# A decoder layer on one core: where TensorE's background jobs stand against the sum of the state in each round of the scan

## The chip, the core and the metric

The kernel runs on one core of one Trainium2 chip. The metric is the device time of one execution in microseconds. The core has TensorE (matmuls and transposes), VectorE, ScalarE, GpSimd and SyncE (which here only issues transfers). Each engine works through its own instructions in order, and they meet through semaphores.

## The reference, cut to what matters

Four sequences of 1024 tokens with 256 channels pass through one decoder layer: two Mamba blocks, a chunked memory read, cross attention and a mixture of eight experts, with layer norms between. The change lies in the Mamba blocks. Their core is

```
def step(h, ins):
    d_t, B_t, C_t, u_t = ins
    dA = exp(d_t[:, :, None] * A)
    h = h * dA + (d_t * u_t)[:, :, None] * B_t[:, None, :]
    y = einsum('bds,bs->bd', h, C_t)
    return (h, y)
...
y = ys + xm * D_ssm
y = y * silu(res)
return y @ out_w.T + out_b
```

with 512 inner channels (four groups of 128) and 16 states per channel. Ahead of the scan stand a norm, the input projection, a causal convolution of four taps, a silu, the projection to x_dbl, and a softplus that gives d_t; behind it stand the gate and the output projection.

## The kernel before, in words

**Items, runs, chunks.** The scan is cut into 16 items: four sequences, two blocks, two halves of 512 tokens. An item has 64 chunks, one for each of the 16 states and four channel groups; a chunk is one scan of 128 channels over 512 tokens. Item i's chunks are numbers 64 i to 64 i + 63, and the stretch in which they are scanned is called a run here. Items 2, 3, 6, 7, 10, 11, 14 and 15 are second halves: their scans start from a carried state.

**Rounds.** TensorE, VectorE, ScalarE and GpSimd all go through the same outer loop over c, one round per chunk (lines 1314, 1727, 1012 and 788). In round c

- TensorE does `fill(c + 2)` (lines 1281 to 1291): four transposes that bring the scan's input, d u B, of chunk c+2 into one of two PSUM banks. It waits until `scanned` shows that scan c is done.
- TensorE does `add_y(c - 6)` (lines 1302 to 1308): four transposes that add the weighed states of chunk c-6 into the four banks that hold y. It waits for GpSimd's `c_weighed` and signals `summed`. In rounds 6 to 9 of a run `open_y` (lines 1293 to 1300) goes before it: eight matmuls that start y with xm times D.
- VectorE does `scan(c)` (lines 1714 to 1725). It waits for `dbu_full` (the fill of c), `da_ready` (ScalarE's decay), and, since the states go to a ring of eight slots, for `summed` of chunk c-8.
- GpSimd does `weigh_c(c - 4)` (line 784), the product of the states with C, and `spread_b` (line 768), which makes input for later fills; ScalarE does `decay(c + 4)` (line 1009) and the other spreads (line 999).

**Jobs.** The work of other items is strewn over the rounds as background jobs. For TensorE they are: transposes and products around the output projection of the item before (`turn_y`, `leave`), transposes of the normed input (`turn_xn`), input and gate projections (`project_in`, line 1246), x and z projections (`project_x`, `project_dt`, lines 1256 and 1271), and transposes of B, C and u. The tables in lines 404 to 424 name the round of each. By its place r among the 64 rounds of a run, TensorE has jobs at r = 3, 4 (transposes of the normed input), 6, 9, 12, 15 (input projection), 23, 24 (x), 26 (B and C), 27, 29, 31, 33 (z), 45, 46, 55, 56 (transposes of u), 46, 49, 52, 55 (transposes of y), 50, 53, 56, 59 (output projection), and 58, 60, 61, 62 (gate). The openings are at r = 6 to 9. Jobs pass through two other PSUM banks, which a planner (lines 433 to 448) assigns ahead of time, by the rounds at which the results are taken by VectorE or ScalarE.

VectorE's own jobs stand behind the scan of their round: the convolution (line 1680) at r = 8 to 19, the softplus and the product with u at r = 37 to 55, the gating and the output rows at r = 47 to 61, and at r = 0, ahead of a second-half item, `sum_halo`: five small operations on the columns at the border of the halves. GpSimd has `find_small` (line 756) at r = 30, 32, 34, 36 and a norm at r = 1.

**Order in a round on TensorE before:** fill, openings, sum, jobs.

Of the kernel before, what the change touches and what calls it, by code (L numbers as in the profile page):

```python
# [39 lines left out]
def decoder_layer(nc, x, ctxT, ctx_mask, norm1_w, norm2_w, in_wT, in_b, conv_w, conv_b, xp_wT, dt_wT, dt_b,  # L40
# [63 lines left out]
    with ExitStack() as ctx:  # L104
# [288 lines left out]
        RUN = ITEMS * CHUNKS  # L393
# [3 lines left out]
        FILL_AHEAD, SUM_AFTER, DECAY_AHEAD, WEIGH_AFTER = 2, 6, 4, 4  # L397
# [57 lines left out]
        def turns_of(c, table):  # L455

            found = [(item_for(c, t), j) for j, t in enumerate(table)]
            return [(i, j) for i, j in found if i is not None]
# [691 lines left out]
        def _(pe):  # L1150
# [90 lines left out]
            def project_in(name, i, f, column, turns, piece):  # L1241
                if piece == 0:
                    pe.wait_ge(bg_by_act, taken("xnT", i, KD - 1))
                    claim_bg(name, i, f)
                for k in part(piece, turns, KD):
                    mm = pe.matmul(psD[:, bg_bank(name, i, f), :], in_w_sb[:, k, column * P:(column + 1) * P], xnT[:, i % 2, k, :],  # L1246
                                   start=k == 0, stop=k == KD - 1)
                    if k == KD - 1:
                        mm.then_inc(bg_full, 1)
# [43 lines left out]
            def open_y(i, f):  # L1293

                if i > 0:
                    pe.wait_ge(y_kept, (i - 1) * KI + f + 1)
                for j in range(JT):
                    mm = pe.matmul(psA[:, f, j * P:(j + 1) * P], xm[:, f, j * P:(j + 1) * P], diag_d[:, f, :],
                                   start=j == 0, stop=False, skip_group_check=True)
                mm.then_inc(opened, 1)  # L1300

            def add_y(c):
                q, n, f = chunk(c)
                pe.wait_ge(c_weighed, c + 1)
                for j in range(JT):
                    mm = pe.matmul(psA[:, f, j * P:(j + 1) * P], h_ring[:, c % H_SLOTS, j * P:(j + 1) * P], ident[:, :],  # L1306
                                   is_transpose=True, start=False, stop=n == NS - 1, skip_group_check=True)
                mm.then_inc(summed, 1)
# [5 lines left out]
            for c in range(-2 * CHUNKS, RUN + TAIL):  # L1314
                if 0 <= c + FILL_AHEAD < RUN:
                    fill(c + FILL_AHEAD)
                for i, f in turns_of(c, OPEN):
                    open_y(i, f)
                if 0 <= c - SUM_AFTER < RUN:
                    add_y(c - SUM_AFTER)  # L1320
                for i, j in turns_of(c, TURN):
                    turn_y(i, j)
                for i, j, piece in pieces_of(c, MO):
                    leave(i, j, piece)
                for i, k in turns_of(c, XNT):
                    turn_xn(i, k)
                for i, f, piece in pieces_of(c, IN):
                    project_in("in", i, f, f, IN[f], piece)
                for i, j, piece in pieces_of(c, [XD]):
                    project_x(i, piece)  # L1330
                for i, j in turns_of(c, [BCT]):
                    turn_bc(i)
                for i, f in turns_of(c, Z):
                    project_dt(i, f)
                for i, f in turns_of(c, UT):
                    turn_u(i, f)
                for i, f, piece in pieces_of(c, GATE):
                    project_in("gate", i, f, KI + f, GATE[f], piece)

            pe.wait_ge(bg_by_dve, taken("mo", ITEMS - 1, JT - 1))  # L1340
            for b in range(B):
# [690 lines left out]
```

## Time and profile before

| | us |
|---|---|
| median of three runs | 3381.56 |
| lowest and highest | 3374.56, 3399.88 |
| the profiled execution, its own time | 3397.87 |
| its span, first to last instruction | 3396.3 |
| busy: TensorE | 2834.2 (83%) |
| busy: VectorE | 2247.4 (66%) |
| busy: ScalarE | 1896.3 (56%) |
| busy: GpSimd | 1912.2 (56%) |
| mean granted TensorE clock, as a share of full speed | 0.93 |

The scan takes the first three fifths of the span: the first scan starts at 91.3 us and the last sum at 2070.4 us. What comes behind (memory read, attention, experts) is not touched by the change. In the scan's stretch from 100 to 2140 us TensorE is busy 1704.65 us, VectorE 1695.05, GpSimd 1601.97 and ScalarE 1558.02, of 2040. The pattern repeats from run to run, so single runs are read below: the seventh item's run, which ends at 1091 us (a second half), and the eighth's behind it, from 1091 to 1215 us (a first half), counting items from 0. Times of single instructions are given from the start of the span; a merged row gives the start of its first instruction and the time to the end of its last.

In the rows, PE is TensorE's matmuls, DVE is VectorE, ACT ScalarE and POOL GpSimd. L1289 is the fill, L1306 the sum, L1723 the scan, L784 the weighing, L768 GpSimd's spread. A bracket at the end of a row gives the engine's idle time before it, in us, and what ended it.

### The profile page before, as it was taken

To read this page: it belongs to the slowest core of one execution; us is meant where nothing else is said; L and a number is where in the kernel's file an instruction comes from. 1 tells how busy PE (TensorE), PEld (TensorE's weight loads), DVE (VectorE), ACT (ScalarE), POOL (GpSimd) and SP (SyncE) were. 2 spreads that over 40 slices of the span, in tenths; PEclk is the share of its full clock that TensorE was granted. 3 is DMA by queue.
4 is the path that set the end of the run, shared out by engine and by line. 5 is a ranking of instruction groups with operands and counts; after the bars stand their busy time and mean duration, and the time that the engine had idled before them with its cause. 6 is when DMAs were issued, how large, how long until landed. Compare 5 with 4: busy or idle time off the path is not lost.

```text
span 3396.3 us, 46777 instructions
## 1 busy us (share of the span) xinstructions
PE 2834.2 (83%) x15574; PEld 2117.4 (62%) x15575; DVE 2247.4 (66%) x3115; ACT 1896.3 (56%) x3225; POOL 1912.2 (56%) x2023
## 2 busy tenths in 40 slices
PE   3878888888888888788788788989897899899995
PEld 1666666666666666666666676657556666566664
DVE  3788888888888888888888983444443433233336
ACT  4877867977877877877877882322322111112114
POOL 1788778878868878778878884011010133333336
PEclk8899899999999999899999998999896799999998
DMA  3011111111111111111111112011002022222114
GB/s 87 26 35 45 32 38 44 35 47 45 47 38 44 32 45 38 36 41 40 37 51 41 43 55 69 1 50 50 16 22 90 25 78 75 101 76 77 46 47 151
DMA packets 115071, 169.62 MB, mean 50 GB/s; under 512 B 16034, under 2 KB 71586, under 8 KB 114882
## 3 DMA queue, kind: packets, MB, share of 16 engines
q1 hardware_dynamic: 96562, 124.63, 12.0%
q0 software_dynamic: 14992, 40.81, 3.5%
q8 instruction: 107, 1.75, 0.2%
q10 hardware_dynamic: 3328, 1.76, 0.2%
q14 instruction: 82, 0.67, 0.1%
HBM read 131.20 MB, written 26.48 MB: 46 GB/s over the span
## 4 chain that ended last, share of the span: by engine, by line
PE 43%; DVE 18%; POOL 16%; issue 13%; DMA 6%; ACT 3%; SPq 0%; POOLq 0%; DVEq 0%; ACTq 0%
POOL arena L784 10%; PE psD L1171 10%; DVE arena L1723 7%; PE psD L1512 5%; PE psD L1289 5%; PE psA L1306 4%; PE psD L1246 4%; POOL arena L768 3%; PE psA L1171 2%; PE psD L1229 2%; POOL arena L756 2%; PE psD L1383 2%; DMA read_w_sb<-arena 2%; DVE arena L1712 2%; PE psD L1404 2%
## 5 line engine op out<-in xcount | busy, mean ns | idle before, releaser
L784 POOL TENSOR_TENSOR arena<-arena 128x512 f32<-128x512 f32 x1024 | 1136.4, 1129 | 13.6 <-DVE arena L1723 3.0
L1289 PE MATMUL psD<-ident,arena 128*128 128x128 f32 x4096 | 679.6, 291 | 239.7 <-DVE arena L1723 227.9
L1289 PEld LDWEIGHTS psD<-ident,arena 128*128 128x128 f32 x4096 | 491.3, 148 | 475.0 <-DVE arena L1723 284.4
L1306 PE MATMUL psA<-ident,arena 128*128 128x128 f32 x4096 | 658.5, 286 | 86.2 <-POOL arena L784 86.1
L1009 ACT ACTIVATE arena<-arena,negA 128x512 f32<-128x512 f32 x1024 | 714.8, 713 | 25.6 <-DVE arena L1723 25.2
L1723 DVE TENSOR_TENSOR_SCAN arena<-arena,carry,psD 128x512 f32<-128x512 f32 x512 | 641.6, 1269 | 110.8 <-PE psA L1306 101.7
L1723 DVE TENSOR_TENSOR_SCAN arena<-arena,psD 128x512 f32<-128x512 f32 x512 | 612.2, 1210 | 129.9 <-PE psA L1306 118.3
L1306 PEld LDWEIGHTS psA<-ident,arena 128*128 128x128 f32 x4096 | 504.1, 148 | 116.6 <-POOL arena L784 114.9
L999 ACT ACTIVATE arena<-arena,bc 128x512 f32<-128x512 f32 x640 | 456.9, 714 | 136.4 <-PE psD L1289 136.4
L768 POOL TENSOR_SCALAR arena<-arena,bc 128x512 f32<-128x512 f32 x384 | 291.5, 759 | 371.0 <-PE psD L1289 316.9
L1171 PE MATMUL psD<-arena 128*128 128x512 f32 (+4 forms) x1128 | 417.9, 512 | 55.2 <-POOL strip L731 30.7
L1109 ACT ACTIVATE in_w_sb<-in_w_sb 128x512 f32<-128x512 f32 x140 | 88.1, 629 | 485.8 <-DVE in_w_sb L1916 480.9
L1171 PEld LDWEIGHTS psD<-arena 128*128 128x128 f32 (+1 forms) x1128 | 208.7, 193 | 174.2 <-issue 155.5
L1512 PE MATMUL psD<-arena 128*128 128x256 f32 x1120 | 261.8, 388 | 2.8 <-DVE arena L1922 2.8
L1246 PE MATMUL psD<-arena,in_w_sb 128*128 128x512 f32 x512 | 242.0, 595 | 3.4 <-DVE halo L1691 2.5
L1512 PEld LDWEIGHTS psD<-arena 128*128 128x128 f32 x1120 | 212.8, 195 | 32.2 <-DVE arena L1922 4.7
L809 POOL TENSOR_TENSOR arena<-arena 128x2048 f32<-128x2048 f32 x4 | 18.1, 4513 | 365.1 <-DMA arena<-in_x 365.1
L1916 DVE TENSOR_TENSOR in_w_sb<-psD,arena 128x512 f32<-128x512 f32 x140 | 96.6, 691 | 175.0 <-PE psD L1171 170.7
L903 ACT ACTIVATE arena<-psA 128x512 f32<-128x512 f32 x144 | 81.4, 596 | 165.9 <-PE psA L1395 56.9
L1680 DVE SCALAR_TENSOR_TENSOR arena<-psD,conv_w_sb,arena 128x511 f32<-128x511 f32 (+2 forms) x192 | 140.1, 730 | 39.0 <-ACT arena L953 38.7
L1929 DVE TENSOR_TENSOR arena<-psD,arena 128x256 f32<-128x256 f32 x70 | 29.7, 424 | 203.4 <-PE psD L1512 203.4
L843 POOL DMA_INDIRECT write_w_sb<-x_dram,read_w_sb x70 | 68.7, 981 | 156.6 <-DMA read_w_sb<-arena 153.6
(244 smaller groups left out, 3755.7 us busy)
## 6 DMA issues: line engine op xcount, KB each, us to landing
arena<-c_dram SPq DMA_DIRECT2D x256, 256.0 KB, 3.3
arena<-in_W POOLq DMA_DIRECT2D x16, 1024.0 KB, 7.2
write_w_sb<-write_w_sb SPq DMA_DIRECT2D x72, 128.0 KB, 2.0
arena<-in_x SPq DMA_DIRECT2D x8, 1024.0 KB, 7.0
arena<-ys_dram SPq DMA_DIRECT2D x16, 512.0 KB, 5.1
arena<-x_dram SPq DMA_DIRECT2D x7, 1024.0 KB, 5.4
x_dram<-arena SPq DMA_DIRECT2D x8, 512.0 KB, 3.1
o_dram<-arena SPq DMA_DIRECT2D x32, 128.0 KB, 1.7
```

Source lines behind the costliest of these rows:

```text
L768: pool.tensor_scalar(g[:, v % 2, j, :], uT[:, i % 2, j, :], bc[:, i % 2, j, n:n + 1], 1.0, ALU.mult, ALU.mult).then_inc(b_by_pool, 1)
L784: pool.tensor_tensor(h_ring[:, c % H_SLOTS, :], h_ring[:, c % H_SLOTS, :], c_rows[:, v % C_SLOTS, :], ALU.mult).then_inc(c_weighed, 1)
L999: act.activation(g[:, v % 2, j, :], uT[:, i % 2, j, :], ACT.Copy, scale=bc[:, i % 2, j, n:n + 1])\
L1009: act.activation(da_ring[:, c % DA_SLOTS, :], dt[:, i % 2, f, :], ACT.Exp, scale=negA[:, f, n:n + 1]).then_inc(da_ready, 1)
L1171: mm = pe.matmul(out_ap, lhs, rhs, start=i == 0, stop=i == len(pairs) - 1)
L1246: mm = pe.matmul(psD[:, bg_bank(name, i, f), :], in_w_sb[:, k, column * P:(column + 1) * P], xnT[:, i % 2, k, :], start=k == 0, stop=k == ...
L1289: mm = pe.transpose(psD[:, c % FILL_BANKS, j * P:(j + 1) * P], g[:, (c // KI) % 2, j, c % KI * P:(c % KI + 1) * P], ident[:, :])
L1306: mm = pe.matmul(psA[:, f, j * P:(j + 1) * P], h_ring[:, c % H_SLOTS, j * P:(j + 1) * P], ident[:, :], is_transpose=True, start=False, sto ...
L1512: mm = pe.matmul(psD[:, 2, 0:D], hidT[:, k, :], w2_sb[:, r, k, :], start=k == 0, stop=k == KH - 1)
L1680: last = dve.scalar_tensor_tensor(xm[:, f, cols:], bank[:, 0:HALF - cols], conv_w_sb[:, f, tap:tap + 1], xm[:, f, cols:], op0=ALU.mult, op ...
L1723: dve.tensor_tensor_scan(h_ring[:, c % H_SLOTS, :], da_ring[:, c % DA_SLOTS, :], psD[:, c % FILL_BANKS, :], 0.0 if h == 0 else carry[:, u, ...
L1916: dve.tensor_tensor(hid[:, n * BANK:(n + 1) * BANK], psD[:, n, :], b1_sb[:, r, n * BANK:(n + 1) * BANK], ALU.add).then_inc(hid_ready, 1)
```

## The change

TensorE's loop body is reordered: the openings and the sum go from behind the fill to the end of the round, behind the jobs. The rounds in which each thing is done, the waits that each carries, and all other engines stay as they are.

```
@@ -1314,10 +1314,6 @@
             for c in range(-2 * CHUNKS, RUN + TAIL):
                 if 0 <= c + FILL_AHEAD < RUN:
                     fill(c + FILL_AHEAD)
-                for i, f in turns_of(c, OPEN):
-                    open_y(i, f)
-                if 0 <= c - SUM_AFTER < RUN:
-                    add_y(c - SUM_AFTER)
                 for i, j in turns_of(c, TURN):
                     turn_y(i, j)
                 for i, j, piece in pieces_of(c, MO):
@@ -1336,6 +1332,10 @@
                     turn_u(i, f)
                 for i, f, piece in pieces_of(c, GATE):
                     project_in("gate", i, f, KI + f, GATE[f], piece)
+                for i, f in turns_of(c, OPEN):
+                    open_y(i, f)
+                if 0 <= c - SUM_AFTER < RUN:
+                    add_y(c - SUM_AFTER)
```

## Rows read from the trace of the kernel before

**Rows 1.** Waits, whole span: us in total, times, longest us.

```profile
PE psD L1289 <- DVE arena L1723: 227.9, 325, 3.4
DVE arena L1723 <- PE psA L1306: 220.0, 258, 1.7
...
PE psA L1306 <- POOL arena L784: 86.1, 92, 1.9
```

**Rows 2.** Busy time by stretch: PE, PEld, DVE, ACT, POOL, clock, DMA share, GB/s.

```profile
1009.00:1030.00 21.00, 20.84 (x128) 14.21 (x126) 16.00 (x14) 20.97 (x36) 18.41 (x18) 1.00 0.18 53
1030.00:1044.00 14.00, 8.60 (x50) 7.28 (x51) 11.74 (x11) 13.94 (x24) 14.00 (x13) 0.79 0.08 19
1044.00:1076.00 32.00, 23.58 (x163) 19.90 (x163) 32.00 (x33) 19.97 (x32) 25.83 (x24) 0.93 0.09 29
```

**Rows 3.** Timeline of TensorE, r23 to r29: start us, us, what.

```profile
1009.90 0.66 PE L1289 MATMUL psD<-ident,arena 128*128 128x128 f32 x4
1010.39 0.60 PE L1306 MATMUL psA<-ident,arena 128*128 128x128 f32 x4
1010.83 1.88 PE L1256 MATMUL psD<-arena,xp_w_sb 128*96 128x512 f32 x4
1012.54 0.60 PE L1289 MATMUL psD<-ident,arena 128*128 128x128 f32 x4
...
1018.57 1.12 PE L1271 MATMUL psD<-arena,dt_w_sb 64*128 64x512 f32 x2
...
1020.55 0.60 PE L1289 MATMUL psD<-ident,arena 128*128 128x128 f32 x4
```

**Rows 4.** Timeline of VectorE, the scan behind the sum of r24.

```profile
1013.62 1.28 DVE L1723 TENSOR_TENSOR_SCAN arena<-arena,carry,psD 128x512 f32<-128x512 f32 x1 [1.20 <-PE psA L1306]
```

**Rows 5.** Timeline of GpSimd, the spread behind the fill of r29.

```profile
1021.25 0.69 POOL L768 TENSOR_SCALAR arena<-arena,bc 128x512 f32<-128x512 f32 x1 [0.52 <-PE psD L1289]
```

**Rows 6.** Timeline of TensorE, two sums that wait for GpSimd, r34 and later.

```profile
1030.68 0.66 PE L1306 MATMUL psA<-ident,arena 128*128 128x128 f32 x4 [0.69 <-POOL arena L784]
...
1035.36 1.12 PE L1306 MATMUL psA<-ident,arena 128*128 128x128 f32 x4 [1.86 <-POOL arena L784]
```

**Rows 7.** Timeline of TensorE, the fills of r50, r56, r58.

```profile
1063.19 0.63 PE L1289 MATMUL psD<-ident,arena 128*128 128x128 f32 x4 [0.36 <-DVE arena L1723]
...
1075.67 0.66 PE L1289 MATMUL psD<-ident,arena 128*128 128x128 f32 x4 [0.20 <-DVE arena L1723]
...
1079.64 0.60 PE L1289 MATMUL psD<-ident,arena 128*128 128x128 f32 x4
```

**Rows 8.** Timeline of VectorE, scans 52, 57 and 58, 0, and 1 on.

```profile
1065.33 1.27 DVE L1723 TENSOR_TENSOR_SCAN arena<-arena,carry,psD 128x512 f32<-128x512 f32 x1
...
1076.12 2.44 DVE L1723 TENSOR_TENSOR_SCAN arena<-arena,carry,psD 128x512 f32<-128x512 f32 x2
...
1091.33 1.22 DVE L1723 TENSOR_TENSOR_SCAN arena<-arena,psD 128x512 f32<-128x512 f32 x1 [1.54 <-PE psA L1306]
1093.92 6.03 DVE L1723 TENSOR_TENSOR_SCAN arena<-arena,psD 128x512 f32<-128x512 f32 x5 [1.37 <-PE psA L1306]
```

**Rows 9.** Timeline of TensorE, the fill of r50 in the next run.

```profile
1186.00 0.63 PE L1289 MATMUL psD<-ident,arena 128*128 128x128 f32 x4 [0.34 <-DVE arena L1723]
```

**Rows 10.** Timeline of VectorE, next run: scan 52, then 0 and 1 around the halo.

```profile
1188.92 1.21 DVE L1723 TENSOR_TENSOR_SCAN arena<-arena,psD 128x512 f32<-128x512 f32 x1
...
1215.06 1.22 DVE L1723 TENSOR_TENSOR_SCAN arena<-arena,psD 128x512 f32<-128x512 f32 x1 [1.60 <-PE psA L1306]
...
1220.40 2.32 DVE L1723 TENSOR_TENSOR_SCAN arena<-arena,psD 128x512 f32<-128x512 f32 x2
```

**Rows 11.** Timeline of TensorE, the fill of r12.

```profile
1115.22 0.66 PE L1289 MATMUL psD<-ident,arena 128*128 128x128 f32 x4 [1.10 <-DVE arena L1723]
```

**Rows 12.** Timeline of VectorE, scans 12 and 14.

```profile
1113.95 1.21 DVE L1723 TENSOR_TENSOR_SCAN arena<-arena,psD 128x512 f32<-128x512 f32 x1
...
1117.76 1.21 DVE L1723 TENSOR_TENSOR_SCAN arena<-arena,psD 128x512 f32<-128x512 f32 x1
```

More of the change, by code:

```diff
@@ L1316, in _ @@
                     fill(c + FILL_AHEAD)
[L1317 to L1320, printed above, removed]
                 for i, j in turns_of(c, TURN):
@@ L1338, in _ @@
                     project_in("gate", i, f, KI + f, GATE[f], piece)
+                for i, f in turns_of(c, OPEN):
+                    open_y(i, f)
+                if 0 <= c - SUM_AFTER < RUN:
+                    add_y(c - SUM_AFTER)
             pe.wait_ge(bg_by_dve, taken("mo", ITEMS - 1, JT - 1))
```

## The prediction

> **What bounds the kernel now.** Engines first. TensorE is the busiest, 83% of the span, with no engine saturated, so the second view is the busy time by stretch [rows 2]. Inside one run of 64 rounds (124 us, from scan(0) at 1091.33 to scan(0) at 1215.06 [rows 8, 10]) the bound moves: from 1009 to 1030 TensorE is busy 20.84 of 21.00 us, from 1030 to 1044 GpSimd 14.00 of 14.00, from 1044 to 1076 VectorE 32.00 of 32.00. A delay handed from one such stretch to the next is kept; one put beside a stretch bound by another engine is lost from sight. Third view, the waits [rows 1]: the scans wait for the sums 258 times, 220.0 us; the fills wait for the scans 325 times, 227.9 us; the sums wait for GpSimd's weighing 92 times, 86.1 us.
>
> So in round c: fill(c+2) needs scan(c), and scan(c+2) needs both fill(c+2) and, through the eight-slot ring of states, the sum of chunk c-6. All are in TensorE's round c, and the sum comes last. It releases the scan now, and the change puts the jobs ahead of it.
>
> **Constants** [rows 3, 4]. Fill and sum each occupy TensorE 0.44 us (the sum starts at 1010.39, the product behind it at 1010.83); a product of four matmuls takes 1.71 (to 1012.54), the shorter one of a z round 1.05 (the row's 1.12 less the overlapped tail), four transposes of a job 0.44, an opening of y 0.89 (eight of the same kind). A scan starts 0.64 after the sum that frees it starts (1012.54 + 0.44 = 1012.98, scan at 1013.62), and takes 1.28 in a run of the second half of a sequence, 1.21 in one of the first [rows 4, 10]. A waiting fill starts 0.06 after its scan ends (scan(12) 1113.95 + 1.21, fill 1115.22 [rows 11, 12]). From a sum to the fill two rounds on is thus 0.64 + 1.28 + 0.06 = 1.98 us. Behind the sum TensorE has sum, fill, sum = 1.32 before that fill. Before, jobs lay in this 1.98; now they lie ahead of it, so a job round followed by a round without one costs up to 0.6 to 0.7. Where the next round has a product too, TensorE is late anyway and the delay is zero.
>
> **Part by part, one run** (r is the round's place among the 64; 38 of the 64 have no job and keep their order).
>
> r23 to r29, x and z products. Before, fill(r23) is at 1009.90. After: product 10.35 to 12.06, sum 12.06, scan(25) 12.70; r24's sum 14.65, scan(26) 15.3 to 16.6, fill(r26) behind it, fill(r27) 18.0, z to 19.5, scan(29) 20.15 to 21.4, fill(r29) 21.5, before 1020.55 [rows 3]: +0.9. There GpSimd takes over: its spread at 1021.25 waits for that fill [rows 5], and it is then busy without a gap until TensorE's sum waits for it at 1030.68 [rows 6]. The two further z rounds (0.55 each) lie beside it and cost nothing; without that cover they cost 1.1. I take 0.9, bounds 0 and 2.0.
>
> r45 to r55, transposes, VectorE-bound: a sum 0.44 later still precedes the scan, since VectorE has jobs of its own between scans and no idle (33 instructions fill 1044 to 1076 [rows 2]). Zero. r50, the output product: fill at 1063.19, sum 1065.35 instead of 1063.66, scan(52) 1066.0 instead of 1065.33 [rows 7, 8]: +0.7 in second-half runs. In the next run (fill 1186.00, scan 1188.92) the same arithmetic gives 1188.8, earlier than that scan starts anyway [rows 9, 10]: zero. 0.7 x 8 runs; bounds 0 and 0.7 x 15.
>
> r56, output product and transposes (2.15): fill 1075.67, sum 1078.27, scan(58) 1078.9 to 1080.2, while before it was the second of two back to back from 1076.12 and over by 1078.56. Fill(r58) moves from 1079.64 to 1080.25: +0.6. Bounds 0 and 0.7.
>
> r58 to r62, four gate products and one output product in consecutive rounds: zero until the last. Before, scan(0) starts at 1091.33 [rows 8], so the sum of r62 at 1090.69; after, the sum is a product later, 1092.4, scan(0) at 1093.05 and scan(1) at 1094.25, before 1093.92: +0.3. At 8 of the run boundaries VectorE sums the halo between those two scans: scan(0) at 1215.06, scan(1) at 1220.40 [rows 10], with nothing idle between. There the whole product, 1.7, goes onto the path: +1.7.
>
> r3 and r4, two sets of transposes: +0.35 at the 8 halo boundaries, nearly 0 at the other 7, where GpSimd holds the sum of r4 anyway. Bounds 0 and 0.44.
>
> r6 to r17, four input products, four openings. The first product and the openings cost 0.3: the scans wait later, but VectorE's wait for ScalarE's last tap now lies beside a scan. At r12: fill 1115.22, sum 1117.4, scan(14) at 1118.0, before 1117.76 [rows 11, 12]: +0.3; r15 the same. Together 0.95, bounds 0 (VectorE's convolution covers all) and 1.3.
>
> **What costs nothing.** No transfer and no other engine's queue is reordered. Ahead of the sum now stand the jobs' own waits; they are short (the product at 1010.83 follows the sum at once, the planner claims banks rounds ahead), and behind them in TensorE's queue wait the sum and through it the scan. Results of jobs come 0.44 us earlier; ScalarE's drains could gain that, and no chain ends on them.
>
> **The sum**, over the 15 runs that have each job:
> 15 x (0.9 + 0.6 + 0.95) = 36.8; r50: 8 x 0.7 = 5.6; r62: 8 x 1.7 + 7 x 0.3 = 15.7; transposes r3, r4: 8 x 0.35 = 2.8. Total +61 us. The profiled execution took 3397.87 us (span 3396.3), so it would be 3459; the median of the three is 3381.56, 16 lower, and the same additions give **3442 us**, +1.8%. With the upper bounds: 15 x (2.0 + 0.7 + 1.3) + 15 x 0.7 + 16.7 + 15 x 0.44 = 94, so 3475. With only r56 and the boundaries: 9 + 16 = 25, so 3406.
>
> **A rule against the row.** TensorE is busiest, yet its waits before the sum fall at r34 to r41 in the two runs I read in full, as at 1030.68 and 1035.36 [rows 6], and these rounds have no job. The Trainium skill, Perfetto Trace Analysis, Identifying the Most-Contended Engine, says to optimise first the engine with the highest occupancy, and its next section to find that engine's gaps and let what ends them come sooner. By that rule, filling TensorE's waits with jobs is a gain, and it is the faster rival below.
>
> **Rivals.**
> 1. *Faster: jobs fill the wait for GpSimd.* The idle before sums is 86.1 us [rows 1]; if it were spread evenly, 26/64 of it, 35 us, would be filled: 3347. It decides if the waits sit in job rounds. For: the wait exists and jobs are independent. Against: the placement above. 7%.
> 2. *No difference: the delays are taken back.* If GpSimd's stretch starts no later and the convolution covers the input products, 25 to 30 us stay: 3408. For: VectorE idles before 1013.62 and GpSimd before 1021.25 [rows 4, 5]. Against: at r29 and at the halo, chains hand over without a gap. 19%.
> 3. *Much slower: the clock falls.* The granted clock is 1.00 from 1009 to 1030 and 0.79 from 1030 to 1044 [rows 2]; after waits and one idle of 1.86 us the sum at 1035.36 takes 1.12 instead of 0.66 [rows 6], which is the level of 1.2 instead of 2.4 GHz. The change opens gaps of 0.6 in stretches that were solid. One fall of two to four rounds among products costs 2.6 each, 5 to 10 us a run: 3442 + 75 to 150, so 3517 to 3592. Against: TensorE stays about 80% busy there (2.8 of 3.5 us in two z rounds), and the fill after an idle of 1.10 at 1115.22 still takes 0.66 [rows 11]. 12%. The Trainium skill, TensorE: Matmul & The Clock Gate, part 1, has the throttled state as the default that activity releases; by that rule new gaps can only cost, and the trace agrees in direction (0.79 where TensorE waits, 1.00 where it is solid).
>
> That the change doesn't act is excluded: 258 scans are released by a sum.
>
> **How the numbers follow.** My forecast 62%, its own range 3415 to 3475. About 1%, 34 us, is what a measurement of this kernel can tell from none. Faster is rival 1, 0.07; within 1% rival 2, 0.19; slower the forecast and rival 3, 0.74. The range 3398 to 3485 leaves out rival 1, the far part of rival 3 and the low edge of rival 2.
>
> **What would show it.** The waits of the scans for the sums should rise from 220 us to 300 or more, and the fills' waits for scans should rise with them; sums' waits for GpSimd should fall by a few us. Fill(r27) to fill(r29) should take about 3.5 us instead of 3.0; scan(0) should still start 0.64 after the sum of r62, with the product now ahead of both. Everything behind the scan should keep its length. I am wrong if a scan in a job round is released by VectorE's own queue more often than I found in two runs, or if the clock in the solid stretches is no longer 1.00.

## The result, and the profile after

The kernel with the new order takes 3451.76 us, the median of four runs (3449.99 to 3453.68). The four runs of the kernel before beside them gave 3399.88, 3374.56, 3381.56 and 3374.64, median 3378.1. The ratio is 1.0207, interval 1.0169 to 1.0245 (medians divided by each other give 1.0218). Measured a second time, six runs gave a median of 3451.43 (3437.25 to 3455.25), ratio 1.0166 (1.0124 to 1.0209) against all runs of before. The two measurements put the cost of the change at 1.7 and 2.1%, and their intervals leave open whether it is above or below 2%. The forecast was 3442 in a range from 3398 to 3485. A few executions lie far above all others at a lower granted clock (as 3611.2 us at 0.813, in the kernel with r62 ahead below); they are in the counts and medians below, but in no ratio.

**What part of it is the change.** Ten of the twelve kernels of this study show two sorts of times, some 15 to 27 us apart (3374 to 3377 and 3400 to 3405 in the ten runs of the kernel before below, 3437 and 3450 to 3455 in the six of the kernel after), and the other two only the longer sort. The difference lies behind the scan: in the three profiles of the shorter sort all but the scan takes 1395.6 to 1402.1 us, in the eleven of the longer 1418.6 to 1426.0. So kernels are compared below by the length of the scan, from the start of the first to the start of the last of the 1024 scans. Of before's first four runs three were of the shorter sort, of after's none, and the 73.7 us between the medians hold some 20 us of this mixture. Sort against sort, the change costs some 50 us in the longer and 60 in the shorter, 1.5 and 1.8%.

| kernel, profiled execution | span | first to last scan | all the rest |
|---|---|---|---|
| before | 3396.3 | 1972.5 | 1423.8 |
| before, a second profile | 3398.0 | 1978.4 | 1419.6 |
| after | 3449.0 | 2030.1 | 1418.9 |
| after, a second profile | 3448.8 | 2030.2 | 1418.6 |

The scan is 54.6 us longer than the mean of the two before (1975.4), and the rest is within 5 us of what it was. The added time is in the scan. The two profiles of the unchanged kernel differ by 5.9 us in the scan, so a difference of that size between two single profiles shows nothing by itself; after's two agree to 0.1.

The busy time of the page after (page, first part) has hardly moved [against the table of before]: TensorE 2841.8 us for 2834.2, GpSimd 1918.3 for 1912.2.

```profile
PE 2841.8 (82%) x15574; PEld 2101.2 (61%) x15575; DVE 2232.2 (65%) x3115; ACT 1900.7 (55%) x3225; POOL 1918.3 (56%) x2023
```

So the time is in waits. The view of waits of after (us in total, times, longest us) answers to [rows 1]:

```profile
POOL arena L768 <- PE psD L1289: 397.2, 164, 4.6
...
DVE arena L1723 <- PE psA L1306: 331.1, 299, 2.9
PE psD L1289 <- DVE arena L1723: 289.1, 449, 3.2
...
PE psA L1306 <- POOL arena L784: 61.6, 75, 1.9
```

The same view of before has this row for GpSimd:

```profile
POOL arena L768 <- PE psD L1289: 316.9, 157, 4.3
```

The scans' wait for the sums rose from 220.0 to 331.1 us and the fills' wait for the scans from 227.9 to 289.1. The sums wait 24.5 us less for GpSimd, but GpSimd waits 80.3 us more for fills. TensorE's wait has moved to the engines behind it.

The place where the first term of the sum was read, r27 to r29 of the same run, now looks like this on TensorE (timeline: start us, us, what, idle before). It answers to [rows 3]:

```profile
1040.02 0.60 PE L1289 MATMUL psD<-ident,arena 128*128 128x128 f32 x4
1040.55 1.12 PE L1271 MATMUL psD<-arena,dt_w_sb 64*128 64x512 f32 x2
1041.60 0.66 PE L1306 MATMUL psA<-ident,arena 128*128 128x128 f32 x4
1042.09 0.60 PE L1289 MATMUL psD<-ident,arena 128*128 128x128 f32 x4
1042.53 0.60 PE L1306 MATMUL psA<-ident,arena 128*128 128x128 f32 x4
1043.63 0.66 PE L1289 MATMUL psD<-ident,arena 128*128 128x128 f32 x4 [0.50 <-DVE arena L1723]
```

The z product stands ahead of the sum, the scan behind that sum starts 0.69 later (1042.29), and the fill of r29 waits for it: 3.61 us from the fill of r27 to that of r29. GpSimd's spread behind it and VectorE's next scan, in the order of their starts, answer to [rows 4, 5]:

```profile
1044.39 0.69 POOL L768 TENSOR_SCALAR arena<-arena,bc 128x512 f32<-128x512 f32 x1 [1.80 <-PE psD L1289]
...
1045.96 2.45 DVE L1723 TENSOR_TENSOR_SCAN arena<-arena,carry,psD 128x512 f32<-128x512 f32 x2 [1.22 <-PE psA L1306]
```

GpSimd's idle ahead of that spread is 1.80 us where it was 0.52.

TensorE's clock did not fall. The whole scan by stretch (length, then busy time of PE, PEld, DVE, ACT and POOL, granted clock, DMA share, GB/s), the kernel before first:

```profile
91.00:2064.00 1973.00, 1650.42 (x10539) 1285.64 (x10538) 1684.57 (x1724) 1553.59 (x2583) 1596.40 (x1660) 0.95 0.14 41
```

and after:

```profile
91.00:2121.00 2030.00, 1663.38 (x10540) 1271.75 (x10539) 1668.95 (x1724) 1557.59 (x2583) 1601.74 (x1660) 0.97 0.13 40
```

From 0.95 to 0.97: TensorE is at its low level for 140 us of the scan (144 in the second profile), where the two profiles of the kernel before have 189 and 203. At the place above, from 1033 to 1043 us, the granted clock is 1.00.

**Where in a run the time went in.** For each place r the start of the scan was compared between the kernels, as a mean over the first 15 runs (us per run, against the mean of the two profiles of before; for r45 to r56 over all eight second-half runs, and over the first-half runs without the first of all, which has 0.66):

| from scan to scan | predicted | measured |
|---|---|---|
| r1 to r22 | 0.95, and 0.35 behind a halo | 1.13 |
| r22 to r45 | 0.9 | 0.67 |
| r45 to r56, second-half runs | 0.7 | 0.65 |
| r45 to r56, first-half runs | 0 | -0.01 |
| r56 to r2 of the next, with the halo | 2.3 | 1.44 |
| r56 to r2 of the next, without | 0.9 | 1.21 |

The means hide a split by halves. From r1 to r22 the first-half runs are 1.60 us longer and the second-half runs 0.60; from r22 to r45 it is 1.23 and 0.02 (1.20 and 0.16 in the second profile of after). Within r45 to r56 the eight second-half runs go from -0.25 to +1.77.

Over 15 runs the measured column gives 17.0 + 10.1 + 5.1 + 8 x 1.44 + 7 x 1.21 = 52.2 us, where the predicted column gives 61. The 2.4 us that are left lie in the first and the last run.

### The profile page after: what moved, and what is told of

Same layout as the page of the kernel before. It is cut to its first block, busy times and chain, and to the rows that moved or that the text cites. A ratio compares the mean times of both kernels' runs of the same rounds, so it can differ in the third digit from the quotient of the medians.

```text
span 3449.0 us, 46777 instructions
## 1 busy us (share of the span) xinstructions
PE 2841.8 (82%) x15574; PEld 2101.2 (61%) x15575; DVE 2232.2 (65%) x3115; ACT 1900.7 (55%) x3225; POOL 1918.3 (56%) x2023
## 4 chain that ended last, share of the span: by engine, by line
PE 46%; DVE 17%; POOL 14%; issue 12%; DMA 6%; ACT 4%; SPq 1%; POOLq 0%; DVEq 0%; ACTq 0%
PE psD L1171 9%; POOL arena L784 9%; DVE arena L1723 8%; PE psD L1289 6%; PE psD L1246 5%; PE psD L1512 5%; PE psA L1306 4%; POOL arena L768 2%; PE psD L1229 2%; PE psA L1171 2%; PE psD L1383 2%; DMA read_w_sb<-arena 2%; POOL arena L756 2%; PE psD L1404 2%; DMA ys_dram<-arena,read_w_sb 1%
## 5 line engine op out<-in xcount | busy, mean ns | idle before, releaser
L1289 PE MATMUL psD<-ident,arena 128*128 128x128 f32 x4096 | 675.4, 290 | 308.3 <-DVE arena L1723 289.1
L1289 PEld LDWEIGHTS psD<-ident,arena 128*128 128x128 f32 x4096 | 477.2, 147 | 442.3 <-DVE arena L1723 342.4
L1306 PE MATMUL psA<-ident,arena 128*128 128x128 f32 x4096 | 649.2, 283 | 61.6 <-POOL arena L784 61.6
L1306 PEld LDWEIGHTS psA<-ident,arena 128*128 128x128 f32 x4096 | 496.1, 146 | 204.3 <-issue 102.3
L840 POOL DMA_DIRECT2D read_w_sb<-arena x70 | 39.8, 569 | 188.4 <-DMA write_w_sb<-write_w_sb 167.3
```

The lines of the kernel that those rows point to most:

```text
L1289: mm = pe.transpose(psD[:, c % FILL_BANKS, j * P:(j + 1) * P], g[:, (c // KI) % 2, j, c % KI * P:(c % KI + 1) * P], ident[:, :])
```

## The experiments

Two theories went into them. **Mine:** a job ahead of the sum delays the scan two rounds on through the ring of states, each stretch that TensorE or a chain through it bounds keeps its own part of the delay, and the parts add up. **The rivals:** jobs ahead of the sum use time in which TensorE waits anyway (faster), or the delay is an effect of the clock or of the mixture of times.

### The kernel before once more

No edit.

> The kernel before, unchanged, profiled once more: its first profiled execution took 3397.87 us, two others of it 3374.6. If that execution had something of its own in the scan, this one shows a scan shorter by some 20 us (1950 instead of 1972 from the first to the last scan) and tells where. If it was longer behind the scan, the scan's rounds are the same to 0.1 us.

Median 3400.67 us of ten runs (3373.74 to 3405.06), ratio 0.9998 (0.9962 to 1.0034). The unchanged kernel itself lands near 3376 or near 3401. Its profile is of the longer sort. The scan did not repeat to the 0.1 us a round that was expected for that case: it is 5.9 us longer than in the first profile, and that in five of the 16 runs, by 0.8 to 2.0 us in four and by -1.0 in one. The profile of the old order with an earlier sum (third experiment) is of the shorter one, and since their program behind the scan is the same, the two can be laid side by side there. First the kernel before, second profile, behind its scan (columns as above):

```profile
2070.00:3398.00 1328.00, 1146.41 (x4938) 810.86 (x4936) 534.88 (x1322) 300.63 (x566) 299.25 (x333) 0.91 0.18 61
2270.00:2570.00 300.00, 276.35 (x1271) 187.41 (x1271) 135.74 (x303) 91.71 (x167) 20.47 (x6) 0.92 0.08 25
2570.00:2870.00 300.00, 250.11 (x1071) 189.34 (x1070) 117.27 (x370) 48.03 (x88) 66.68 (x83) 0.82 0.20 70
```

then the third experiment's kernel:

```profile
2060.00:3370.00 1310.00, 1126.11 (x4931) 794.06 (x4929) 535.92 (x1321) 299.88 (x566) 296.79 (x333) 0.92 0.19 62
2260.00:2560.00 300.00, 269.49 (x1291) 184.47 (x1290) 143.03 (x329) 92.45 (x170) 23.72 (x13) 0.96 0.09 26
2560.00:2860.00 300.00, 250.76 (x1098) 184.56 (x1097) 114.58 (x352) 48.61 (x91) 69.42 (x84) 0.86 0.21 75
```

TensorE is busy 20 us longer for the same program, and the clock is 0.92 and 0.82 in two stretches of 300 us where the other has 0.96 and 0.86 (these are cut by time and hold some tens of instructions more or fewer). Over all 14 profiles the mean granted clock behind the scan is 0.92 to 0.93 in the three of the shorter sort and 0.90 to 0.91 in the eleven of the longer. What decides between the sorts was not found.

### The new order once more

No edit to the kernel after.

> The changed kernel once more, timed in more rounds. The kernel before shows times of two sorts, near 3377 and near 3401, and the profiles put the 20 us between them behind the scan (1308 to 1312 us or 1328 to 1332 us from the last scan on). If that is so, the changed kernel has both sorts too, near 3430 and near 3452, its four times so far were all of the longer sort, and the ratio of all runs comes down from 1.0207 to 1.015 to 1.017. Its scan is 2030 us again, within 6. Rival: it is always near 3452 and the ratio stays at 1.02.

Median 3451.43 us of six (3437.25 to 3455.25), ratio 1.0166 (1.0124 to 1.0209), scan 2030.2 us. The result stands, the scan repeats to 0.1 us, and two of the six runs (3437.25 and 3437.39) are of a shorter sort, as was expected.

### More slack in the ring, new order

```
-        FILL_AHEAD, SUM_AFTER, DECAY_AHEAD, WEIGH_AFTER = 2, 6, 4, 4
+        FILL_AHEAD, SUM_AFTER, DECAY_AHEAD, WEIGH_AFTER = 2, 5, 4, 4
...
-        XB, OPEN = 1, [6, 7, 8, 9]
+        XB, OPEN = 1, [5, 6, 7, 8]
```

on the kernel after. The sum of chunk c-5 then stands in round c, and frees the slot of scan(c+3) instead of scan(c+2).

> New order, but the sum is that of chunk c-5 instead of c-6, and the openings one round earlier (r5 to r8). The scan of c+2 then needs the sum of the round before, which is always issued before the jobs of this round. My theory (the jobs delay the sum, the ring of eight slots hands that to the scan): the waits of the scans for the sums fall from 331 to under 80 us and the time comes back to 3370 to 3400 us. Rival A (the new order costs by itself, through TensorE's gaps or its clock): it stays at 3440 to 3455. Rival B (GpSimd's weighing is only one round ahead now): the sums' wait for GpSimd rises from 62 to 150 us or more, and half of the gain is lost again, 3410.

Median 3379.09 us of ten (3356.88 to 3384.12), ratio 0.9953 (0.992 to 0.9987); scan 1956.0 us, 74.1 shorter than after's. Its waits:

```profile
POOL arena L768 <- PE psD L1289: 338.7, 154, 3.7
DVE arena L1723 <- PE psD L1289: 228.9, 281, 1.6
...
PE psD L1289 <- DVE arena L1723: 182.7, 256, 3.4
```

No scan waits for a sum any more: the 331.1 us of after are gone from the view, and the scans now wait for their fills. The whole loss of the new order hangs on the release of the ring by a sum two rounds ahead of its scan. The sums themselves wait more for GpSimd, 116.6 us for 61.6: the rival had that direction right, though not its 150 us nor the half of the gain that it was to cost.

### More slack in the ring, old order

The same two lines changed in the kernel before.

> Old order (fill, openings, sum, jobs) with the sum of chunk c-5 and the openings one round earlier. My theory: here the scan was released by the sum 0.44 us behind the fill; now by the fill. Where the scans waited for sums behind a product (220 us in all) they still wait for the fill, 0.44 earlier: 3350 to 3380 us. Rival B (GpSimd only one round ahead): the sum now waits in front of the jobs, 3385 to 3400.

Median 3393.32 us of ten (3367.62 to 3398.2), ratio 0.9996 (0.9959 to 1.0032); scan 1968.0 us. The slack by itself gives 7.4 us of scan in the old order against the mean of before's profiles. That is not much more than these differ among themselves, but sort by sort the times are 6 to 9 us shorter too (3367.62 to 3371.8 and 3393.12 to 3398.2 us). The 3350 to 3380 us that were expected are missed by the median, which lies where the rival had it, and the sums' wait for GpSimd rises from 86.1 to 114.0 us, as the rival says. In its waits, too, the scans wait for fills and not for sums:

```profile
DVE arena L1723 <- PE psD L1289: 215.9, 251, 3.3
...
PE psD L1289 <- DVE arena L1723: 187.5, 255, 3.4
```

With one round of slack the new order is the shorter one, by 12.0 us of scan (1956.0 against 1968.0). The times agree, sort by sort: 3356.88 to 3357.1 and 3377.43 to 3384.12 against 3367.62 to 3371.8 and 3393.12 to 3398.2 us. So the faster rival exists, on another kernel: once no scan hangs on the sum, its place behind the jobs is a gain. Of the 12 us 5.2 lie at r6 to r12, among openings and input products, and two single runs (3.4 and 2.7 us) hold much of the rest. What makes it there was not taken further.

### The addition of the bias moved away from the halo, new order

```
-        XB, OPEN = 1, [6, 7, 8, 9]
+        XB, OPEN = 20, [6, 7, 8, 9]
```

on the kernel after. GpSimd's addition of the bias (line 737), which for half of the items stands at r1, beside the halo, goes to r20.

> New order; GpSimd adds the output bias to the input rows (2.4 us) at r20 instead of r1. At r0 the five small halo operations of VectorE stand beside that addition in 4 of the 8 runs that have them: scan 0 to scan 1 takes 4.3 us there and 2.4 to 2.5 in the other 4. Theory (VectorE's operations on SBUF wait while GpSimd's run): the 4.3 becomes 2.5 in those 4 runs, other runs keep theirs, and the time falls by 4 x 1.8 = 7 us at most, to 3445. Rival (the 4.3 has to do with the runs' place): unchanged.

Median 3441.51 us of five (3419.56 to 3443.56), ratio 1.0137 (1.0086 to 1.0189); scan 2019.7 us, 10.4 shorter than after's. The reason to try it stands in VectorE's halo behind item 8's run [rows 10]. The kernel before, VectorE's operations of the halo:

```profile
1216.59 1.14 DVE L1563 TENSOR_TENSOR halo_tmp<-halo,conv_w_sb 128x8 f32<-128x8 f32 x2
...
1217.76 2.72 DVE L1568 TENSOR_TENSOR halo_sum<-halo_sum,halo_tmp 128x8 f32<-128x8 f32 x2
```

and GpSimd beside them:

```profile
1215.55 2.15 POOL L784 TENSOR_TENSOR arena<-arena 128x512 f32<-128x512 f32 x2
...
1217.66 2.35 POOL L737 TENSOR_TENSOR arena<-arena,out_b_sb 128x1024 f32<-128x1024 f32 x1
```

After, VectorE:

```profile
1245.29 1.22 DVE L1723 TENSOR_TENSOR_SCAN arena<-arena,psD 128x512 f32<-128x512 f32 x1 [1.37 <-PE psA L1306]
1246.42 0.14 DVE L1559 TENSOR_TENSOR halo_sum<-halo,conv_w_sb 128x12 f32<-128x12 f32 x1
1246.48 2.40 DVE L1563 TENSOR_TENSOR halo_tmp<-halo,conv_w_sb 128x8 f32<-128x8 f32 x2
1248.92 0.78 DVE L1568 TENSOR_TENSOR halo_sum<-halo_sum,halo_tmp 128x8 f32<-128x8 f32 x2
1249.62 2.32 DVE L1723 TENSOR_TENSOR_SCAN arena<-arena,psD 128x512 f32<-128x512 f32 x2
```

and GpSimd:

```profile
1246.41 2.37 POOL L737 TENSOR_TENSOR arena<-arena,out_b_sb 128x1024 f32<-128x1024 f32 x1
```

This experiment, VectorE:

```profile
1242.34 0.14 DVE L1559 TENSOR_TENSOR halo_sum<-halo,conv_w_sb 128x12 f32<-128x12 f32 x1
1242.40 0.45 DVE L1563 TENSOR_TENSOR halo_tmp<-halo,conv_w_sb 128x8 f32<-128x8 f32 x2
1242.89 0.87 DVE L1568 TENSOR_TENSOR halo_sum<-halo_sum,halo_tmp 128x8 f32<-128x8 f32 x2
1243.68 4.79 DVE L1723 TENSOR_TENSOR_SCAN arena<-arena,psD 128x512 f32<-128x512 f32 x4
```

The two L1563 operations are the same in all three: eight columns, 0.45 us when only the short operations of GpSimd's norm (line 748) run with them, and 2.40 when the bias addition started 0.07 ahead of them; they end at 1248.88, 0.10 behind that addition (1248.78). The operation at L1559, which starts within 0.01 us of the addition, is not delayed (0.14 us in both). From scan(0) to scan(1) it is 5.3 us before, 4.3 after and 2.5 with the addition moved, at exactly the boundaries that had the addition (runs 1, 2, 9 and 10; starts of scans, us):

| boundary behind run | 0 | 1 | 4 | 5 | 8 | 9 | 12 | 13 |
|---|---|---|---|---|---|---|---|---|
| before | 5.57 | 5.28 | 3.49 | 3.43 | 5.34 | 5.28 | 3.49 | 3.42 |
| after | 4.34 | 4.26 | 2.47 | 2.40 | 4.34 | 4.27 | 2.47 | 2.40 |
| bias at r20 | 2.48 | 2.41 | 2.48 | 2.42 | 2.48 | 2.42 | 2.48 | 2.42 |

Four boundaries give 4 x 1.86 = 7.4 us, the 7 that were expected. The other 3.0 of the 10.4 are what is left of 4.7 us gained at r2 to r22 and 1.4 lost at r22 to r45, with no cause found. The Trainium skill, SBUF — State Buffer, Who interferes with whom, has VectorE and GpSimd share a pair of ports under an exclusive lock: an operation of VectorE with two inputs in SBUF contends with one of GpSimd that reads SBUF, and the order of issue decides which of them is held up. The 2.40 against 0.45 us agree with it.

### One kind of job ahead of the sum at a time

All from the kernel before. Fill, openings and sum stay as they are, and the named loops move from behind the sum to between fill and openings; for x, z and the transposes of B and C:

```
                     fill(c + FILL_AHEAD)
+                for i, j, piece in pieces_of(c, [XD]):
+                    project_x(i, piece)
+                for i, j in turns_of(c, [BCT]):
+                    turn_bc(i)
+                for i, f in turns_of(c, Z):
+                    project_dt(i, f)
                 for i, f in turns_of(c, OPEN):
                     open_y(i, f)
                 if 0 <= c - SUM_AFTER < RUN:
                     add_y(c - SUM_AFTER)
```

> Only the x, B/C and z jobs (r23 to r33) ahead of the sum, all others behind it. By my terms the scan is 15 x 0.9 = 14 us longer than in the kernel before (1972 to 1978), so 1989; by the trace of the changed kernel, in which r23 to r45 takes 0.6 more a run, 9 us. If GpSimd's stretch hid all: 0. If it hid none of the z rounds: 30.

Median 3410.78 us of eight (3391.47 to 3414.26), ratio 1.0035 (1.0 to 1.007); scan 1990.5, +15.1 on the mean of before. Between r22 and r45 each run is 0.75 us longer, where the full change has 0.67. Its waits:

```profile
PE psD L1289 <- DVE arena L1723: 272.1, 404, 3.4
DVE arena L1723 <- PE psA L1306: 244.6, 258, 1.8
PE psA L1306 <- POOL arena L784: 61.4, 70, 1.9
```

The sums' wait for GpSimd falls from 86.1 to 61.4, as much as in the full change, and yet the scan is 15.1 us longer: this is the faster rival at its best place, and it loses. Its clock in the scan is 0.97, as in the full change. The 0.75 is again split, 1.23 in first-half runs and 0.18 in second-half ones.

The output projection and the gate (`leave`, `project_in("gate", ...)`) moved in the same way:

```
                     fill(c + FILL_AHEAD)
+                for i, j, piece in pieces_of(c, MO):
+                    leave(i, j, piece)
+                for i, f, piece in pieces_of(c, GATE):
+                    project_in("gate", i, f, KI + f, GATE[f], piece)
```

> Only the output projection and the gate products (r50 to r62) ahead of the sum. My terms: 5.6 (r50) + 9 (r56) + 15.7 (r62 with the halo) = 30 us on the scan. By the trace of the changed kernel the halo step was given back in part (scan 0 to scan 1 is 1.0 to 1.2 shorter there, and 1.35 shorter where there is no halo), so 5.6 + 9 + 8 x 0.7 + 7 x 0.3 = 22 us.

Median 3418.26 us of eight, seven of them from 3411.53 to 3421.72, the longer sort, and one of 4781.15; ratio 1.0073 (1.0038 to 1.0109); scan 1991.7, +16.3, so less than either of the two sums, 30 and 22. From r56 to r2 of the next run +1.09 us with the halo and +0.87 without, each 0.34 or 0.35 less than in the full change. From r50 to r53, where the product of r50 lies, the second-half runs are 0.24 us longer in the mean, and seven of the eight by at most 0.31, for the 0.7 of the prediction.

The input projection:

```
                     fill(c + FILL_AHEAD)
+                for i, f, piece in pieces_of(c, IN):
+                    project_in("in", i, f, f, IN[f], piece)
```

> Only the input projection (r6, r9, r12, r15) ahead of openings and sum. My term: 15 x 0.95 = 14 us on the scan. If VectorE's convolution covered it: 0. If the whole 0.6 to 0.7 of each of four rounds went onto the path: 40.

Median 3411.95 us of eight (3389.41 to 3417.95), ratio 1.0037 (1.0002 to 1.0072); scan 1990.3, +14.9. From r1 to r22 each run is 1.06 us longer. The scans wait 268.6 us for sums in it, for 220.0.

The transposes of y and of the normed input:

```
                     fill(c + FILL_AHEAD)
+                for i, j in turns_of(c, TURN):
+                    turn_y(i, j)
+                for i, k in turns_of(c, XNT):
+                    turn_xn(i, k)
```

> Only the transposes of y (r46 to r55) and of the normed input (r3, r4) ahead of the sum. My terms: 2.8 us on the scan (0.35 at 8 run boundaries), against scans of 1972.5 and 1978.4 in the two profiles of the kernel before: 1975 to 1981. The three parts already run add 15, 16 and 15 us to the mean of those two and the whole change 55, so if the parts are additive 9 us are left for this one: 1984.

Median 3403.38 us of eight (3399.14 to 3407.01), ratio 1.0037 (1.0008 to 1.0065), though all eight were of the longer sort and before's were mixed; scan 1976.6, +1.2, within what before's profiles differ. Those jobs of 0.44 us cost next to nothing.

The four parts add up to 15.1 + 16.3 + 14.9 + 1.2 = 47.5 of the 54.6 us. The other 7 are the openings, the transposes of u, and what parts do together, and none of these was run alone; 5 of the 7 lie between r56 and r2 of the next run, where the transposes of u at r56 are the one job that the full change moves and the four parts do not. The loss is many small delays that are kept, and no single place holds it.

### The last rounds apart: r58 to r61, and r62

The sum goes behind the jobs in these rounds alone:

```
+                late = c % CHUNKS in (58, 59, 60, 61)
...
-                if 0 <= c - SUM_AFTER < RUN:
+                if 0 <= c - SUM_AFTER < RUN and not late:
                     add_y(c - SUM_AFTER)
...
+                if 0 <= c - SUM_AFTER < RUN and late:
+                    add_y(c - SUM_AFTER)
```

> Only in r58, r59, r60 and r61 do the jobs stand ahead of the sum; each of these rounds is followed by another with a product. My theory: TensorE is late anyway, so the scan's length is that of the kernel before, 1972 to 1979 us. Rival (each product ahead of a sum costs 0.4 to 0.7 wherever it stands): 15 x 4 x 0.55 = 33 us more, 2008.

Median 3400.67 us of eight (3373.35 to 3408.9), ratio 1.0003 (0.9965 to 1.0041). From r56 to r2 of the next run it is +0.32 us with the halo and 0.00 without. Products in consecutive rounds are nearly free, as the prediction had it.

The same with `late = c % CHUNKS == 62`:

> Only in r62, the last product before rounds without one, does the job stand ahead of the sum. My prediction gave 1.7 at the 8 boundaries with the halo and 0.3 at the 7 others, 15.7 us. The trace of the changed kernel says that VectorE's halo operations wait for GpSimd and give 1.0 back: 8 x 0.7 + 7 x 0.3 = 7.7 us. In this kernel scan 0 to scan 1 should take 2.4 instead of 3.5 us at the boundaries 5, 6, 13, 14 and 4.3 instead of 5.3 to 5.6 at 1, 2, 9, 10.

Median 3402.8 us of eight (3379.32 to 3411.07, and one of 3611.2), ratio 1.0009 (0.9972 to 1.0045). From r56 to r2 of the next it is +0.45 with the halo and +0.43 without. The 1.7 us at the halo are not there. At these boundaries scan(0) to scan(1) takes 4.31, 4.01, 2.22, 2.17, 4.09, 4.02, 2.22 and 2.17 us, 1.3 less than in the kernel before: scan(0) comes a product later, and three quarters of that are given back in the halo.

The boundaries add 2.5 and 6.6 us, and both kernels have a longer scan than that: 1983.8 and 1985.1 us, +8.4 and +9.7 on the mean of before (+5.4 and +6.7 on its second profile), the first outside the 1972 to 1979 that were expected. Some of this is what the unchanged kernel differs by, and some is TensorE's clock, away from the edit. In the second one's run 4, at r20 and on, with the scan at line 1726 (start us, us, what):

```profile
634.66 1.06 PE L1289 MATMUL psD<-ident,arena 128*128 128x128 f32 x4 [1.62 <-DVE arena L1726]
635.51 1.06 PE L1306 MATMUL psA<-ident,arena 128*128 128x128 f32 x4
636.36 1.06 PE L1289 MATMUL psD<-ident,arena 128*128 128x128 f32 x4
637.22 1.06 PE L1306 MATMUL psA<-ident,arena 128*128 128x128 f32 x4
638.07 0.66 PE L1289 MATMUL psD<-ident,arena 128*128 128x128 f32 x4
```

and the same place in the kernel before:

```profile
631.08 0.66 PE L1289 MATMUL psD<-ident,arena 128*128 128x128 f32 x4 [1.61 <-DVE arena L1723]
631.58 0.60 PE L1306 MATMUL psA<-ident,arena 128*128 128x128 f32 x4
```

Behind an idle of the same length four groups of transposes take 1.06 us at the lower of the two levels here and 0.60 to 0.66 there, and up to r56 this run is 1.6 us longer than before's. In the scan TensorE is at its low level for 189 and 203 us in the two profiles of the kernel before, 199 and 216 in these two, and 140 in the one with x and z ahead. So the clock is shown at this place, and as the cause of the whole excess it is not shown.

### Slack, new order and the bias at r20 together

```
-        FILL_AHEAD, SUM_AFTER, DECAY_AHEAD, WEIGH_AFTER = 2, 6, 4, 4
+        FILL_AHEAD, SUM_AFTER, DECAY_AHEAD, WEIGH_AFTER = 2, 5, 4, 4
...
-        XB, OPEN = 1, [6, 7, 8, 9]
+        XB, OPEN = 20, [5, 6, 7, 8]
```

on the kernel after.

> New order with the sum of chunk c-5 (scan 1956 us) and GpSimd's bias addition at r20. If the two gains add: scan 1956 less 4 x 1.8 = 1949 us, and the time 0.7% to 0.9% under the kernel before (ratio 0.992). If the halo is hidden behind the gate products here: 1956 and 0.995.

Median 3346.95 us of six (3341.99 to 3370.55), ratio 0.9898 (0.9855 to 0.9941) against the kernel before; scan 1944.8 us, 30.6 shorter than before's. It is shorter than both kernels; against the one before by 1.0%, with an interval from 0.6 to 1.5. Against the one with slack and new order alone the bias gives 11.2 us of scan, as it gave 10.4 on the kernel after. The remaining 19.4 are slack and order, of which 7.4 are slack by itself.

## Why the prediction was right, and where it was not

**The mechanism** was right: a sum behind a job frees the scan two rounds later too late, and the fill two rounds on, with GpSimd's spread behind it, inherits the delay. The waits that it named rose as it said (331.1 us, where 300 or more was asked; fills' waits 227.9 to 289.1), and with one round more in the ring the waits for sums and the loss are both gone. The sums' wait for GpSimd fell by 24.5 us, where a few were said. The size of the sum, 61 us for 54.6, is right in part by luck: several of its terms are off, and their errors cancel.

**r23 to r29**, 0.9 a run. The arithmetic at the place is right, 3.61 us from fill to fill where about 3.5 was said, and 11.89 from the fill of r23 to that of r29 (1031.74 to 1043.63) for 11.6 said and 10.65 before. What was said of the stretch behind it is not. The two further z rounds do delay the scans there: in the run in which the term was read, the delay since scan 22 is 1.77 us at scan 29, 2.16 at scan 31 and 3.60 at scan 35. Then nearly all of it is given back, to 0.44 at scan 45, in that run and in the mean over all to 0.67 (0.75 with this part alone). That mean is 1.23 in first-half runs and 0.02 in second-half runs, so the 0.9, read in a second-half run, came near it by luck. The stretch that gives it back runs in this run from scan 31 to scan 45 (windows, columns as above), in the kernel before:

```profile
1021.95:1051.40 29.45, 21.42 (x124) 16.39 (x123) 25.65 (x23) 29.31 (x49) 29.45 (x25) 0.83 0.10 31
```

and after:

```profile
1045.96:1073.69 27.73, 20.87 (x124) 15.28 (x122) 24.63 (x22) 27.46 (x46) 27.73 (x24) 0.88 0.09 29
```

GpSimd is busy without a gap in both, as the prediction said, but ScalarE is as full (29.31 of 29.45 us), and already in [rows 2] it has 20.97 of 21.00 where the prediction names TensorE alone. Which of the two takes the delay back, and why only second-half runs lose all of it, stays open.

**r45 to r55**, zero for the transposes, 0.7 for r50 in second-half runs alone: 0.65 there and -0.01 in first-half runs. The split by halves came from reading two neighbouring runs that differ only in the length of their scan, and it holds in the mean. The size does not rest on r50: with the output products and the gate alone ahead, r50 to r53 gives 0.24, so the product costs about a third of what was said, and the 0.65 is the mean of runs from -0.25 to 1.77 in which other delays arrive too (with x and z alone ahead the same stretch gives 0.38).

**r56**, 0.6. In the same run the fills of r56 and r58 on TensorE are now

```profile
1099.79 0.65 PE L1289 MATMUL psD<-ident,arena 128*128 128x128 f32 x4 [0.20 <-DVE arena L1723]
1100.29 1.89 PE L1229 MATMUL psD<-out_w_sb,arena 128*128 128x256 f32 x8
1102.01 0.60 PE L1278 MATMUL psD<-ident,arena 128*128 128x128 f32 x4
...
1104.52 0.63 PE L1289 MATMUL psD<-ident,arena 128*128 128x128 f32 x4 [0.59 <-ACT arena L999]
```

4.73 us apart against 3.97 [rows 7], so +0.76 for +0.6. What r56 to r2 adds in the full change, less what r58 to r61 and r62 add alone, is 1.44 - 0.32 - 0.45 = 0.67 with the halo and 1.21 - 0.43 = 0.78 without. Without the transposes of u, in the kernel with output and gate products ahead, the same difference is 0.32 and 0.44.

**r62 and the halo: the term that was mis-sized.** The prediction had: "There the whole product, 1.7, goes onto the path", at 8 boundaries, 13.6 us. Alone it measured 0.45, so 3.6 us. Scan(0) does start a product later, and 0.64 behind the sum, as said: the sum of r62 starts at 1244.65 and the scan at 1245.29:

```profile
1244.65 0.60 PE L1306 MATMUL psA<-ident,arena 128*128 128x128 f32 x4
```

But the time from scan(0) to scan(1) was taken as fixed because VectorE had no idle in it. Most of those 5.3 us was VectorE waiting inside its own instructions for GpSimd's, which stand in the profile as busy time: before, L1563 ends at 1217.73 beside a weighing that ends at 1217.70, and L1568, 2.72 us for two operations on eight columns, ends at 1220.48 behind the addition that ends at 1220.01. After, the halo meets the addition alone, and 1.0 us comes back (1.3 with r62 alone). The seven boundaries without a halo cost 0.43 instead of 0.3.

**r3, r4 and r6 to r17**, 0.35 and 0.95: 1.13 a run over the whole stretch, 1.06 with the input products alone, but 1.60 in first-half runs and 0.60 in second-half ones (1.51 and 0.54 with the input products alone), so the one figure of 0.95 was between two, and 1.2 us in all for the transposes of y and the normed input.

Terms were off in both directions, and that they add up so closely is luck: r62 at the halo by 10 us and r23 to r29 by 3.4 too much, the rest by 5 too little, and the sum of +61 stands against +54.6 of scan, 2.4 of it in the first and last runs. The forecast of 3442 for the median is 10 us under the measured one since it started from a before whose runs were mostly of the shorter sort; the sum from the profiled execution, 3459, is 8 over its counterpart, 3450.63.

**The rivals.** *Faster* fell: filling TensorE's wait for GpSimd is worth nothing while the scan waits for the same sum. The placement, read in two runs, was a right reason against it, but not the whole one, for with x and z ahead 24.7 us of that wait did go and the scan still grew by 15.1. With a round more in the ring the rival does hold, by 12.0 us of scan. The Trainium skill, Perfetto Trace Analysis, Optimization Strategy, would have what blocks the busiest engine's gaps start sooner or end faster. It does not speak of filling a gap with other work, which is what the prediction made of it and what the change does; here that did not help until the ring had room. *No difference* fell: between r31 and r45 most of a delay of 3.5 us is taken back, in second-half runs all of it, but elsewhere too little is, and 54.6 us stay where the rival had 25 to 30. *The clock falls* had the sign wrong: the granted clock in the scan rose from 0.95 to 0.97. Where gaps of 0.6 us came into the stretch that was solid, it stayed at 1.00, and long waits became fewer; the sums' wait for GpSimd, behind which [rows 6] show the fall to 1.12 us, went from 92 times to 75.

## What to carry to other kernels

In an engine's queue the order within a round decides which consumer is late: put first what frees a slot of a ring that somebody waits for, and background work behind it, or give the ring a round more and the order is free; here the new order costs 55 us of scan without this round and, by single profiles, gains 12 with it. When a chain has no idle, ask of each instruction in it whether its duration fits its size, for a wait inside an instruction counts as busy and will shrink or grow when its neighbour moves. When a term is read in one kind of run, read it in the other kind too: two of the means here are of halves that differ by 1 us. Where one kernel has two sorts of times, compare stretches between the same two instructions of their traces before medians are believed to the last 20 us.

## What the runs showed of the hardware

- Two operations of VectorE on 128x8 took 0.45 us with no bias addition of GpSimd's beside them, and 2.40 us when GpSimd had started a 2.37 us addition just ahead; moving that one addition 19 rounds away gives 10.4 us of scan with the sum of chunk c-6 and 11.2 with that of chunk c-5, both in the new order.
- One program has times some 25 us apart (3376 and 3401 for the kernel before). In profiles of two kernels with the same program behind the scan, one of each sort, this part takes 1328 against 1310 us, with TensorE busy 1146.41 against 1126.11 us and a mean clock there of 0.91 against 0.92.
- From scan 31 to scan 45 ScalarE and GpSimd are both 99% busy or more. A delay of the scans that has grown to 3.5 us by scan 35 is down to 1.2 us at scan 45 in one kind of run and to nothing in the other. Two full engines did not mean that the stretch hands on what it gets.
- After an idle of 1.6 us TensorE came back at its higher level in one kernel (0.66 us for four transposes) and at its lower in another (1.06), with the nearest edited round 22 rounds earlier. What is the same locally need not cost the same.
